# A post-LayerNorm transformer block on one core: attention state kept transposed, 4-bit grid by one integer operation, a new order of all four engines

## What is computed

```python
x = _layernorm(x + _L0_attn_ref(x, ...))
x = _layernorm(x + _L0_ffn_ref(x, ...))
x = _layernorm(x + _L1_attn_ref(x, ...))
x = _layernorm(x + _L1_ffn_ref(x, ...))
```

```python
q = _apply_rope(_rmsnorm(q, norm_w), cos, sin)
k = _apply_rope(_rmsnorm(k, norm_w), cos, sin)
scores = jnp.einsum('bqhd,bkhd->bhqk', q, k)
pattern = jnp.square(scores / D_HEAD) * causal
z = jnp.einsum('bhqk,bkhd->bqhd', pattern, v).reshape(B, S, D_MODEL)
return x + z @ Wo.T * SCALE
```

```python
scale = jnp.max(jnp.abs(xb), axis=-1, keepdims=True) / 6.0
scale = jnp.maximum(scale, jnp.float32(1e-12))
xn = xb / scale
idx = jnp.searchsorted(_MID, jnp.abs(xn))
q = _GRID[idx] * jnp.sign(xn) * scale        # _GRID = 0, .5, 1, 1.5, 2, 3, 4, 6
```

## Time and profile before

| | |
|---|---|
| time, median of 3 runs | 256.37 us (256.21 to 257.42) |
| the profiled execution | 256.5 us, of which 254.7 us span from its first to its last instruction |
| DVE | busy 215.4 us, 85% of the span, 533 instructions |
| PE | busy 213.5 us, 84%, 1840 matmuls; weight loads 160.8 us |
| ACT | busy 129.4 us, 51% |
| POOL | busy 91.1 us, 36% |
| granted TensorE clock | 0.96 on the mean |
| DMA | 5.97 MB, busy in the first 13 us, then little |

### The profile page before, as it was taken

One profiled execution on the slowest core, in us unless ns is written; L12 is line 12 of the kernel. 1 busy time (PEld: TensorE's weight loads), 2 busy tenths in 40 slices (PEclk: granted clock), 3 DMA queues, 4 the chain that ended last, 5 costly groups with the idle time before them and its releaser, 6 DMA issues.

```text
span 254.7 us, 5368 instructions
## 1 busy us (share of the span) xinstructions
PE 213.5 (84%) x1840; PEld 160.8 (63%) x1840; DVE 215.4 (85%) x533; ACT 129.4 (51%) x242; POOL 91.1 (36%) x124
## 2 busy tenths in 40 slices
PE   0675776886898999998999997999899999997751
PEld 0232654753765877686887676687577898885631
DVE  0599999999969998898999899999899989964252
ACT  0387258546229548834236478644782333644330
POOL 4008128034110912471210256673255234141241
PEclk9979799899599999999999999999999999999997
DMA  7900010010000000000000000000000000000001
GB/s 221 350 5 0 3 42 0 4 41 0 3 0 24 21 3 21 3 1 4 1 3 0 0 23 1 3 0 23 0 4 1 3 0 21 3 21 22 3 22 41
DMA packets 6074, 5.97 MB, mean 23 GB/s; under 512 B 1440, under 2 KB 5408, under 8 KB 6048
## 3 DMA queue, kind: packets, MB, share of 16 engines
q1 hardware_dynamic: 5184, 4.99, 6.1%
q10 hardware_dynamic: 864, 0.65, 0.8%
HBM read 4.58 MB, written 1.05 MB: 22 GB/s over the span
## 4 chain that ended last, share of the span: by engine, by line
DVE 30%; issue 28%; PE 24%; POOL 13%; ACT 2%; DMA 2%; DVEq 1%; POOLq 1%; SPq 0%; ACTq 0%
POOL pat L2032 5%; POOL ln_rstd L2000 4%; PE psum L325 4%; DVE x L1279 4%; PE psum L465 3%; PE psum L494 2%; PE psum L447 2%; POOL ln_veps L1995 2%; DVE val L1172 2%; PE psum L357 2%; DMA bqkv<-in_b_qkv 2%; PE psum L586 2%; DVE rope_b L1336 2%; PE psum L504 1%; DVE val L1189 1%
## 5 line engine op out<-in xcount | busy, mean ns | idle before, releaser
L2032 POOL TENSOR_SCALAR_AFFINE_SELECT pat<-pat 128x1024 f32<-128x1024 f32 x32 | 43.9, 1392 | 45.6 <-ACT pat L795 45.6
L795 ACT ACTIVATE pat<-psum 128x1024 f32<-128x1024 f32 x32 | 31.1, 1020 | 16.3 <-PE psum L406 16.1
L1995 POOL TENSOR_TENSOR ln_veps<-ln_mv,ln_eps 128x2 f32<-128x2 f32 x32 | 8.6, 271 | 77.6 <-DVE ln_mv L1273 77.6
L1279 DVE TENSOR_SCALAR x<-y,ln_mv,ln_rstd 128x128 f32<-128x128 f32 x64 | 23.1, 408 | 6.9 <-POOL ln_rstd L2000 6.9
L2000 POOL TENSOR_TENSOR ln_rstd<-ln_veps,minus_half 128x2 f32<-128x2 f32 x32 | 23.7, 745 | 1.9 <-POOL ln_veps L1995 0.2
L447 PE MATMUL psum<-pat,v_wide 128*32 128x128 f32 x512 | 18.4, 304 | 5.7 <-POOL pat L2032 4.3
L406 PE MATMUL psum<-q_wide,k_t 32*128 32x512 f32 x128 | 18.2, 638 | 4.2 <-ACT pat L795 1.8
L447 PEld LDWEIGHTS psum<-pat,v_wide 128*32 128x32 f32 x512 | 16.4, 124 | 7.8 <-issue 7.5
L357 PE MATMUL psum<-wqkv,xt_in 128*128 128x384 f32 x32 | 14.5, 591 | 6.5 <-DMA bqkv<-in_b_qkv 5.9
L795 ACT ACTIVATE x_t<-psum 128x256 f32<-128x256 f32 x16 | 6.1, 385 | 24.9 <-PE psum L331 24.5
L325 PE MATMUL psum<-w_sb,h 128*128 128x128 f32 x128 | 16.2, 280 | 2.8 <-ACT h L795 2.0
(11 more groups left out here) (123 smaller groups left out, 497.1 us busy)
## 6 DMA issues: line engine op xcount, KB each, us to landing
xt_in<-in_x_t SPq DMA_DIRECT2D x8, 128.0 KB, 3.5
x_in<-in_x SPq DMA_DIRECT2D x8, 128.0 KB, 3.2
out_dram<-x SPq DMA_DIRECT2D x8, 128.0 KB, 1.7
w_sb<-in_w SPq DMA_DIRECT2D x2, 256.0 KB, 3.8
gu_raw<-in_w_gu ACTq DMA_DIRECT2D x1, 384.0 KB, 3.8
keys<-in_keys_t SPq DMA_DIRECT2D x1, 256.0 KB, 3.9
values<-in_vals SPq DMA_DIRECT2D x1, 256.0 KB, 4.3
wqkv<-in_w_qkv_t SPq DMA_DIRECT2D x1, 192.0 KB, 3.9
```

The source lines that it names most:

```text
L795: return nc.scalar.activation(dst, src, func, **kw)
L1279: op = dve.tensor_scalar(dst[:, b * D:(b + 1) * D], y[:, b * D:(b + 1) * D], ln.mv[:, b, 0:1], ln.rstd[:, b:b + 1], ALU.subtract, ALU.mult)
L2032: pool.affine_select(out=part, in_=part, compare_op=ALU.is_ge, fill=0.0, base=0, pattern=[[0, 2 * HG], [1, P]], channel_multiplier=-1).the ...
```

## The change

Five things are changed together.

1. **State transposed.** `add_state` takes v as the stationary operand (32 columns) and the features as the moving one, so the state comes out transposed; `take_state` masks it into `state_t`, a new PE stage `turn_state` (three transposes) and a new ACT stage `copy_state` turn it back, and `z_state` waits for `copy_state`. `scale_v` writes v contiguous to `v_sc`, and a new ACT stage `spread_v` spreads it into `v_wide`; `z_pattern` waits for `spread_v`.
2. **Grid by one integer operation.** `quant_power` goes; `quant_grid` is one AND and OR on the integer bits, and the float factor moves into the add and the subtract, which become scalar_tensor_tensor operations with an int32 tile as one input.
3. **Fourth LayerNorm in place.** `y4` goes; `ln4_in` writes `x4`, and waits for the store of two steps before.
4. **Order.** The lists of all engines, `BANK` and `PSUM_TURNS` are new.
5. **Start.** Nine matmuls of a zeroed tile into an unused part of PSUM bank 0 stand ahead of `project(0)`; `project(0)` waits for the weights alone, and the bias has a semaphore of its own that `bias_qk(0)` waits for.

```diff
-QUANT_STEPS = 10
+QUANT_STEPS = 9
-ROUND = 1.5 * 2.0 ** 22
+GRID_BITS = 0x40800000
+GRID_BASE = 0x20000000
+GRID_STEP = 85.0 / 32.0 * 2.0 ** -8
-PSUM_TURNS = (("project", 0), ("project", 1), ("transpose_qk", 0), ("project", 2), ("scores0", 0), ("transpose_rq",
+PSUM_TURNS = (("project", 0), ("project", 1), ("transpose_qk", 0), ("project", 2), ("scores0", 0), ("transpose_qk",
...
-            sp.dma_start(bqkv[:, :], b_qkv[:, :]).then_inc(ld["qkv"], 16)
+            sp.dma_start(bqkv[:, :], b_qkv[:, :]).then_inc(ld["bias"], 16)
...
+            def keep_warm(n):
+                pe.wait_ge(s["cleared"], 1)
+                for _ in range(n):
+                    pe.matmul(psum[:, 0, STATE_W:STATE_W + P], x3_t[:, 0:P], x3_t[:, 0:P], start=True, stop=True)
+            keep_warm(9)
...
-                    pe.wait_ge(ld["qkv"], 32)
+                    pe.wait_ge(ld["qkv"], 16)
...
-                wait(pe, "take_state", u - 1)
+                wait(pe, "copy_state", u - 1)
...
-                pe.wait_ge(s["scale_v"], u + 1)
+                pe.wait_ge(s["spread_v"], u + 1)
...
-                        pe.matmul(psum[:, 0, 32 * n:32 * n + 32], feats[u % 2][:, 1, b, gr * P:(gr + 1) * P],
-                                  v[:, gr * HG:(gr + 1) * HG, :], start=(u == 0 and n == 0), stop=(u == PAIRS - 2),
-                                  skip_group_check=True)
-                    half = slice(b * NH * HALF, (b + 1) * NH * HALF)
-                    mm = pe.matmul(psum[half, 0, STATE_A:STATE_W], last[u % 2][:, 1, b, :], v, start=False,
-                                   stop=(u == PAIRS - 2), skip_group_check=True)
+                        at_b = b * P + 32 * gr
+                        pe.matmul(psum[32 * gr:32 * gr + 32, 0, b * P:(b + 1) * P], v_sc[u % 2][:, at_b:at_b + 32],
+                                  feats[u % 2][:, 1, b, gr * P:(gr + 1) * P], start=(u == 0 and b == 0),
+                                  stop=(u == PAIRS - 2), skip_group_check=True)
+                for b in range(B):
+                    half = STATE_A + b * NH * HALF
+                    mm = pe.matmul(psum[:, 0, half:half + NH * HALF], v_sc[u % 2][:, b * P:(b + 1) * P],
+                                   last[u % 2][:, 1, b, :], start=False, stop=(u == PAIRS - 2), skip_group_check=True)
+            def turn_state(u):
+                pe.wait_ge(s["take_state"], u + 1)
+                bank_free(pe, "turn_state", u)
+                for n in range(STATE_W // P):
+                    mm = pe.transpose(at("turn_state", u)[:, n * P:(n + 1) * P], state_t[:, n * P:(n + 1) * P], ident[:, :])
...
+            def spread_v(u):
+                act.wait_ge(s["scale_v"], u + 1)
+                wait(act, "z_pattern", u - 2)
+                act_op(v_wide[u % 2][:, :, :, :].rearrange("p b g (h r) -> p (b g h) r", r=32 + DH)[:, :, 0:DH],
+                       v_sc[u % 2][:, :].rearrange("p (n e) -> p n e", e=DH), ACT.Copy).then_inc(s["spread_v"], 1)
+            def copy_state(u):
+                act.wait_ge(s["turn_state"], u + 1)
+                wait(act, "z_state", u - 1)
+                act_op(state[u % 2][:, :], at("turn_state", u)[:, 0:STATE_W], ACT.Copy).then_inc(s["copy_state"], 1)
...
-                dve.tensor_scalar(q.mag.bitcast(I32), q.val.bitcast(I32), 0x7F800000, None,
-                                  ALU.bitwise_and).then_inc(q.step, 1)
-                dve.tensor_scalar(q.mag, q.mag, 1.0, ROUND, ALU.max, ALU.mult)\
+                dve.tensor_scalar(q.mag, q.val.bitcast(I32), GRID_BITS, GRID_BASE, ALU.bitwise_and, ALU.bitwise_or)\
-                dve.tensor_tensor(q.val, q.val, q.mag, ALU.add).then_inc(q.step, 1)
+                dve.scalar_tensor_tensor(out=q.val, in0=q.mag, scalar=GRID_STEP, in1=q.val, op0=ALU.mult, op1=ALU.add)\
-                dve.tensor_tensor(q.val, q.val, q.mag, ALU.subtract)\
+                dve.scalar_tensor_tensor(out=q.val, in0=q.mag, scalar=-GRID_STEP, in1=q.val, op0=ALU.mult, op1=ALU.add)\
...
-                wait(dve, "ln4_out", u - 1)
-                dve.tensor_tensor(y4[:, :], at("ffn_down", u)[:, 0:T], x3_b2[:, :], ALU.add).then_inc(s["ln4_in"], 1)
+                if u >= 2:
+                    dve.wait_ge(stored[u % 2], 16 * (u // 2))
+                dve.tensor_tensor(x4[u % 2][:, :], at("ffn_down", u)[:, 0:T], x3_b2[:, :], ALU.add).then_inc(s["ln4_in"], 1)
...
+            dve.memset(x3_t[:, 0:P], 0.0).then_inc(s["cleared"], 1)
```

More of the change, by code:

```diff
@@ L623, in _ @@
[L623 to L629 removed]
+            project(4)
+            transpose_qk(2)
+            transpose_feats(1)
+            transpose_last(1)
+            add_state(1)
+            transpose_qk(3)
+            z_state(1)
+            scores0(2)
+            transpose_rq(1)
+            z_pattern(1)
+            turn_gate_up(0)
+            output_projection(1)
@@ L656, in _ @@
-            z_pattern(3)
+            transpose_x2(0)
+            project(7)
+            key_scores(0)
+            add_state(4)
+            transpose_xq(2)
+            transpose_feats(4)
+            gate(2)
+            sum_squares(0)
+            up(2)
+            mean_squares(0)
+            z_state(4)
+            scores0(5)
+            transpose_rq(5)
             transpose_x2(1)
-            transpose_xq(2)
-            mean_squares(0)
+            z_pattern(4)
             key_scores(1)
-            output_projection(3)
@@ L690, in _ @@
+            weigh_values(1)
+            ffn_up(0)
+            scores0(6)
+            z_state(5)
+            turn_state(5)
+            z_pattern(5)
+            scores1(6)
             ffn_down(0)
-            transpose_x3(1)
             transpose_x2(2)
-            transpose_feats(5)
+            output_projection(5)
+            transpose_h(3)
             key_scores(2)
-            add_state(5)
-            ffn_up(1)
+            mlp_down(3)
+            transpose_xq(4)
+            transpose_feats(6)
@@ L735, in _ @@
+            scores1(7)
+            weigh_values(3)
+            ffn_down(1)
+            transpose_rq(7)
+            z_state(7)
+            transpose_x3(2)
+            z_pattern(7)
+            transpose_xq(6)
+            transpose_h(5)
+            output_projection(7)
+            gate(6)
             transpose_x2(4)
-            up(5)
-            scores0(7)
+            mlp_down(5)
+            up(6)
+            ffn_up(2)
             key_scores(4)
-            scores1(7)
+            transpose_x2(5)
```

1366 lines of the change are left out of this document (659 added, 707 removed).

## The result

| | before | after |
|---|---|---|
| time, median of 3 runs | 256.37 us | 225.47 us (224.23 to 225.54) |
| ratio | | 0.877, 95% interval 0.871 to 0.883 |
| profiled execution, span | 254.7 us | 223.8 us |

A forecast was written before the change was run, and what follows sets the result against it. DVE, busy for 94% of the middle, was taken as the bound, with a chain at the end. From the 254.7 us span, -1.5 -7 -3.8 -4 +4 gave 242.4 span, 244.2 us; range 236 to 254.

The forecast's parts named there:

- Start, -1.5: Start of the kernel: DVE fills its wait for the projection with the maximum of the weights, saving 1.45 us later.
- the doubt: At the start: doubtful that the nine matmuls matter, since without them a cold projection would end at 8.3, just in time.
- One operation fewer, -7: Rounding on DVE: AND and multiply merge into one operation, saving 7 us; the two scalar_tensor_tensor operations cost nothing extra.
- the first rival: Rounding on DVE: scalar_tensor_tensor passes twice over its elements, adding 18.1 us of DVE, 262 us in all; chance 0.09.
- Masks, -4: DVE operations held up beside POOL's masks: the new order's longer runs of PSUM reads or reductions give cover, saving 4 us.
- The ceiling of 8.4: Masks: excess of mean over median in four groups of DVE operations, 8.4 us, of which half was taken.
- State, 0: Transposed state: about 1 us times 7 steps saved on PE, the less full engine, none counted; up to 7 as bound.
- Work moved behind the last `hq`, -3.8: Middle of the kernel: 15 normalization instructions at 0.254 us now come after the last 4-bit tile of step 7.
- end, +4: Behind the last `hq`: 8 us more PE work, two places on the chain at about 2 each; between 0 and 8.
- Fourth norm in place, 0: Fourth LayerNorm: `ln4_in` instead of `ln4_out` now waits for a store of two steps before, priced at 0.
- The third: Middle of the kernel: masks hidden entirely, 4.4 us more, and 4 us of DVE's waits gone; 236 us, chance 0.14.
- The second: New stages are waited for: `z_pattern` behind `spread_v` in ACT's queue, 11.2 us given back, 255.4 us; chance 0.11.

## Why the prediction was wrong

- **Start, -1.5: right in the trace, too small to find in the time,** and the doubt was right. The bias is at 8.07 (8.3 forecast) with 0.95 us of work in the gap. No run shows that the projection needs the nine matmuls to be in time: without them the bias is at 8.05. Of its two prices for them the cold one, 5.9 us, was off: the 18 records took 3.68 us, from 1.11 on, and ended before the weights were there.
- **One operation fewer, -7: right in size.** 8.6 in the new order, with 512 ns for the select and 878 and 886 for the two others; the first rival (a second pass, 262 us) is dead. By the sentence of the Trainium skill that stood beside it (Vector Engine (DVE) Microarchitecture Reference, "Points that are easy to get wrong") the operation should have halved its throughput; the trace has none of it with a float32 and an int32 tile (878 and 886 ns, as the plain add of two float32 tiles). In the old order the same edit is worth 3.7. DVE's busy time fell by 5.5 there, to 209.9; where the rest went wasn't tested.
- **Masks, -4: the first step that failed.** They gave 11.6. Two things were wrong in it. The ceiling of 8.4 was the excess of four groups, but 215.4 - 195.1 = 20.3 us of DVE's busy time hung on the masks: many groups that I did not add up had a few long ones each. Nor did the four go as I thought: the three on 128x704 lost their excess, and the normalization, 4.2 of the 8.4, kept most of it (412 ns). And I halved it because "when a mask starts is set by ACT's square, not by DVE's list". That is true and no reason: the change wrote all four lists anew, and both orders are fixed, so an order can put reductions and PSUM reads where the squares end. The second order excerpt showed just that and I gave it half.
- **State, 0: the second step that failed.** The prediction asked what waits the state adds and costed its PE work (about 1 us a step, which is right: the records of `add_state` and `turn_state` add up to 13.6 us, those of `add_state` to 20.8 before and 22.5 in the new order with the old state, so 1.0 to 1.3). It didn't ask which wait it removes: with `v_sc` in between, `scale_v` no longer waits for `z_pattern`. Put back into the changed kernel, that wait costs 4 to 6 of the 6.5 us; the rest is open. The kernel before has no such wait (0.0 in its row). The new order makes it (3.3 us), and the state removes it.
- **Work moved behind the last `hq`, -3.8, and end, +4: the tail about right.** It is 34.35 (36 forecast), with 7.0 us more of PE's work in it (8 forecast) and 2.2 more of DVE's (3.8). That the rest of the order came to nothing net was wrong: it is worth 4.5 without masks, and where these lie wasn't tested.
- **Fourth norm in place, 0:** not tried by itself; the parts leave 0.3 us over for it and others, which is within what they can tell.
- **Rivals.** The third (masks under entirely, and PE's relief reaching DVE) was right on the masks and on DVE's waits for PE, but not on the cause of these, and its 236 came from the same ceiling of 8.4 and from waits already visible. The second did not happen in the new order; its kind did in the old one.

By the terms: 11.6 instead of 4 for the masks, 6.5 instead of 0 for the state, 8.6 instead of 7 for the grid, 4.5 gained instead of 0.2 lost for the rest of the order, and nothing that can be told instead of 1.5 for the start (what the order gives there is in its 4.5). That is 31.2 for 12.3, some 18.9 us more; the miss is 244.2 - 225.5 = 18.7. With each term good to 2 us, the closeness is partly luck.

## What to carry to other kernels

Where an operation on one engine holds up another's, price it over all operations that ran beside it (how far busy time falls when it is left out is the honest ceiling), and look at what kind of work an order lays beside it: a new order can take most of it away without making one instruction shorter. Of a buffer that is put between two stages, ask which wait it removes as well as which it adds; in a reordered kernel that can be a wait which the old trace never showed. And an edit's price belongs to its order: the same grid gave 3.7 or 8.6 us, and the same state 6.5 us gained or 36 lost, by the order and by where its stages stood.

## What was unexpected

- A mask of POOL on 128x1024 held DVE operations on SBUF tiles by 0.8 to 0.9 us, but not PSUM reads, reductions, LayerNorm statistics or reciprocals, and in the old order that came to 15.0 us of 256.4, with 44 us of masks.
- From 20 to 24 us PE was busy throughout at a granted clock of 0.50, after 4 us with 2.11 us of PE; lifting it to 1.00 with idle matmuls changed nothing that could be measured. A stretch at 0.50 from 72 to 76 us, in another execution, was followed by a wait of 2.18 us on DVE: of these two stretches at 1.2 GHz only the later one cost DVE anything.
- 7.8 us of additional matmuls in the changed kernel cost about 1 us (nothing to 3), although PE was busy for 89% of the span.
